# Edge attributes of a graph-attention loop: read by tile number straight from the input, instead of from a staged copy

## The reference

```
x_l = (x @ W_l.T + b_l).reshape(n, 4, 64)
x_r = (x @ W_r.T + b_r).reshape(n, 4, 64)
e_feat = (e_attr @ W_e.T).reshape(-1, 4, 64)
s = leaky_relu(x_l[src] + x_r[dst] + e_feat, 0.2)
alpha = einsum('ehc,hc->eh', s, att)
amax = segment_max(alpha, dst); ex = exp(alpha - amax[dst])
alpha = ex / (segment_sum(ex, dst)[dst] + 1e-16)
out = segment_sum(alpha[..., None] * x_l[src], dst) + bias
h = x + silu(out)
```

## Time and profile before

| what | value |
|---|---|
| time, median of 3 runs | 3392.98 us (3388.5 to 3393.57) |
| the profiled execution, first to last instruction | 3546.6 us |
| edge loop in that execution | about 105 to 1520 us |
| PE busy in the span | 3206.4 us (90%) |
| DVE, ACT, POOL busy | 51%, 39%, 34% |
| bytes moved by DMA in the span | 345.09 MB, 97 GB/s |
| a staged gather, and a store of what it fetched | 56 rows, 448 KB each, 15 times each for both inputs |

### The profile page before, as it was taken

The page is one execution under the profiler, slowest core; times in us unless marked ns, Lnnn a source line. Parts: engine busy times, 40 slices in busy tenths (PEclk is TensorE's granted clock), DMA queues, the critical chain, the costliest instruction groups (busy, mean ns, idle before and its releaser), DMA issues. The chain is left out here.

```text
span 3546.6 us, 52145 instructions
## 1 busy us (share of the span) xinstructions
PE 3206.4 (90%) x14480; PEld 2570.5 (72%) x14481; DVE 1826.2 (51%) x3687; ACT 1387.4 (39%) x4710; POOL 1196.3 (34%) x1148
## 2 busy tenths in 40 slices
PE   6789999999989998957899899889999989999989
PEld 5567776766767676636777777777777778888878
DVE  5666666766766766767353644544373424111002
ACT  2056666666666666663122212312232211222222
POOL 4556666666666666403110310120020001222200
PEclk9899999999999999978999999999999979999999
DMA  7556666665666665533010101000100042333341
GB/s 228 143 146 149 153 149 151 148 147 147 144 147 152 146 149 151 111 100 80 22 43 26 30 8 36 27 8 1 39 24 14 1 156 63 118 117 116 123 134 44
DMA packets 288629, 345.09 MB, mean 97 GB/s; under 512 B 155176, under 2 KB 213655, under 8 KB 284512
## 3 DMA queue, kind: packets, MB, share of 16 engines
q1 hardware_dynamic: 232813, 174.79, 18.5%
q0 software_dynamic: 53632, 157.89, 17.4%
q10 hardware_dynamic: 2064, 10.81, 1.0%
HBM read 298.03 MB, written 44.37 MB: 97 GB/s over the span
## 5 line engine op out<-in xcount | busy, mean ns | idle before, releaser
L1429 POOL DMA_INDIRECT a_g<-xl_d,a_ix x480 | 475.9, 991 | 297.1 <-remote 135.5
L1446 PE MATMUL a_pS<-g_xr,a_lt 128*128 x1680 | 534.8, 401 | 42.5 <-issue 19.4
L1454 PE MATMUL b_pM<-b_m,b_oh 128*112 128x281 f32 x1680 | 457.9, 413 | 23.1 <-DVE g_acc L1585 16.7
L1578 DVE SCALAR_TENSOR_TENSOR a_r<-a_pS,g_attx 128x528 f32<-128x528 f32 x420 | 288.5, 700 | 344.3 <-remote 269.8
L1541 ACT ACTIVATE b_m<-a_g,c_pcx 128x64 f32<-128x64 f32 x1856 | 455.6, 333 | 2.3 <-issue 1.9
L1429 POOL DMA_INDIRECT XS<-xl_d,a_ix x344 | 337.1, 980 | 202.8 <-issue 86.7
L1446 PEld LDWEIGHTS a_pS<-g_xr,a_lt 128*128 128x128 f32 x1680 | 310.3, 193 | 119.6 <-issue 67.2
L1454 PEld LDWEIGHTS b_pM<-b_m,b_oh 128*112 128x112 f32 x1680 | 294.2, 180 | 136.6 <-issue 39.8
L125 POOL TENSOR_TENSOR m_rstd<-m_ve,m_mhalf 125x5 f32<-125x5 f32 x41 | 48.0, 1170 | 902.8 <-DVE m_ve L111 902.8
L1541 ACT ACTIVATE b_m<-XS,c_pcx 128x64 f32<-128x64 f32 x1424 | 349.0, 333 | 1.2 <-issue 1.2
L424 PE MATMUL m_pH<-m_h,m_w 128*128 128x312 f32 (+1 forms) x1280 | 341.9, 428 | 7.7 <-DVE m_h L572 7.7
(11 more groups left out here) (399 smaller groups left out, 4412.6 us busy)
## 6 DMA issues: line engine op xcount, KB each, us to landing
a_db<-dl_d SPq DMA_DIRECT2D x212, 224.0 KB
f_w<-in_ffn_W1p SPq DMA_DIRECT2D x32, 1024.0 KB
m_w<-in_mix_W SPq DMA_DIRECT2D x8, 1024.0 KB
f_w<-in_ffn_W2p SPq DMA_DIRECT2D x8, 1024.0 KB
a_g<-xl_d,a_ix POOLq DMA_INDIRECT x480
a_lt<-eat_d SPq DMA_DIRECT2D x214, 32.0 KB
eat_d<-a_stage SPq DMA_DIRECT2D x15, 448.0 KB
ea_d<-a_stage SPq DMA_DIRECT2D x15, 448.0 KB
```

Source lines behind the costliest of these rows:

```text
L1429: p.indirect_dma_start(out=gathered(t)[:, j, :], out_offset=None, in_=xl_d, in_offset=bass.IndirectOffsetOnAxis(ap=IX[:, t // BSTEPS, n:n ...
L1446: pe.matmul(o, lt[:, j, :], XRW[:, bass.ds(ws[h], 1), :].rearrange("p a d -> p (a d)"), start=True, stop=False)
L1454: ins = pe.matmul(pM[0:WN, h, 0:MW], OH[:, b, j, :], M[:, b, j, :], start=(j == 2 * h), stop=(j == 2 * h + 1))
L1578: v.scalar_tensor_tensor(out=R[:, 2 * h:2 * h + 2, :], in0=pS[0:TE, 2 * h:2 * h + 2, 0:GD], scalar=0.0, in1=attx[:, :].unsqueeze(1).broadc ...
```

## The change

The staged copy goes. The table of tile numbers is loaded once, in the setup, into one row of SBUF (`g_tl`, by way of `tl_d`). In the edge loop SyncE reads the tile number of each pair's first item from that row into a register (`value_load`) and issues a DMA that takes two neighbouring tiles of the input: two DMAs of 16 KB in the place of one of 32 KB, for the transposed attributes and for the others alike. The setup's two gathers and two stores of 1 MB each go, and so do, from each round, the load of 56 tile numbers, the two gathers, the two stores and the waits on them. The input has one tile of padding more. The semaphores `a_eat` and `b_ea` count 32 a step instead of 16.

```diff
--- before
+++ after
...
+        TL = kept("g_tl", [1, ITEMS], I32)
...
-                sp.dma_start(tl_d[0:ITEMS].rearrange("(c p) -> c p", p=128), turned[CH:2 * CH, :]).then_inc(s["i_stored"], 16)
+                sp.dma_start(tl_d.rearrange("(c p) -> c p", p=128), turned[CH:2 * CH, :]).then_inc(s["i_tl_d"], 16)
...
                 xl_part(3)
+                sp.wait_ge(s["i_tl_d"], 16)
+                sp.dma_start(TL[0:1, :], tl_d.unsqueeze(0)).then_inc(s["i_tl"], 16)
...
-                    if q == NG - 2:
-                        a.wait_ge(s["i_ea"], 32)
-                        a.dma_start(eat_d[0:128, :], eaT[:, :]).then_inc(s["i_ea_out"], 16)
-                        a.dma_start(ea_d[0:128, :], ea[:, :]).then_inc(s["i_ea_out"], 16)
...
-                    elif k == 1:
-                        at = bass.IndirectOffsetOnAxis(ap=tile_i[:, 0:1], axis=0)
-                        p.indirect_dma_start(out=eaT[:, :], out_offset=None, in_=g["eaT"], in_offset=at).then_inc(s["i_ea"], 16)
-                        p.indirect_dma_start(out=ea[:, :], out_offset=None, in_=g["ea"], in_offset=at).then_inc(s["i_ea"], 16)
...
+                    def tiles_of(base, c, h):
+                        at = IG * (base + c) + 2 * h
+                        tile = sp.value_load(TL[0:1, (slice(at, at + 1) if isinstance(at, int) else bass.ds(at, 1))], min_val=0, max_val=NTE)
+                        return bass.ds(tile, 2)
+
                     def attributes_of(base, c, k):
-                        sp.dma_start(LT[WN:128, k, :, :], eat_d[four(base, c), :].rearrange("i (c e) -> c i e", c=ED)).then_inc(s[f"a_eat{k}"], 16)
+                        for h in range(2):
+                            sp.dma_start(LT[WN:128, k, 2 * h:2 * h + 2, :],
+                                         g["eaT"][tiles_of(base, c, h), :].rearrange("i (c e) -> c i e", c=ED)).then_inc(s[f"a_eat{k}"], 16)
+
+                    def features_of(base, c, k):
+                        for h in range(2):
+                            sp.dma_start(M[:, k, 2 * h:2 * h + 2, EA0:EA0 + ED],
+                                         g["ea"][tiles_of(base, c, h), :].rearrange("i (e c) -> e i c", c=ED)).then_inc(s[f"b_ea{k}"], 16)
...
-                        if exists(base, t, 0) and t == TILES_AT:
-                            wait(sp, "s_gathered", 32 * i, 0)
-                            sp.dma_start(TIX[:, :], tl_d[staged(i)].unsqueeze(1)).then_inc(s["s_tiles"], 16)
-                        elif exists(base, t, 0) and t == STORE_AT:
-                            sp.wait_ge(s["s_gathered"], 32 * i + 32)
-                            sp.dma_start(eat_d[staged(i), :], STG[:, 0, :]).then_inc(s["s_staged"], 16)
-                            sp.dma_start(ea_d[staged(i), :], STG[:, 1, :]).then_inc(s["s_staged"], 16)
-                        elif exists(base, t, 0) and t == RING - attributes_ahead:
-                            wait(sp, "s_staged", 32 * i, 0)
...
                         if exists(base, t, -WEIGH):
                             wait(sp, "b_summed1", base, t - WEIGH - 1)
-                            sp.dma_start(M[:, t % 2, :, EA0:EA0 + ED], ea_d[four(base, t - WEIGH), :].rearrange("i (e c) -> e i c", c=ED)).then_inc(s[f"b_ea{t % 2}"], 16)
+                            features_of(base, t - WEIGH, t % 2)
...
-                        if t == GATHER_AT:
-                            p.wait_ge(s["s_tiles"], 16 * i + 16)
-                            wait(p, "s_staged", 32 * i, 0)
-                            p.sem_inc(s["a_seen"], 1)
-                            for n, a in enumerate((g["eaT"], g["ea"])):
-                                p.indirect_dma_start(out=STG[:, n, :], out_offset=None, in_=a,
-                                                     in_offset=bass.IndirectOffsetOnAxis(ap=TIX[:, 0:1], axis=0)).then_inc(s["s_gathered"], 16)
...
-                            pe.wait_ge(s[f"a_eat{t % LTS}"], 32 * i + 16 * (t // LTS) + 16)
+                            pe.wait_ge(s[f"a_eat{t % LTS}"], 64 * i + 32 * (t // LTS) + 32)
...
-    ea = np.pad(a["edge_attr_16"], ((0, spare), (0, 0))).reshape(tiles, TE, ED)
+    ea = np.pad(a["edge_attr_16"], ((0, spare + TE), (0, 0))).reshape(tiles + 1, TE, ED)

```

More of the change, by code:

```diff
@@ L48 @@
 ITEMS = 128 * CH
-RI = IG * RING
-STAGED = RI * (ROUNDS + 2)
 ZSLOTS = NT * D // (IG * GD)
@@ L809, in graph_attention @@
 def graph_attention(nc, s, zone, XS, ident, x, xn_d, g, sums_d, scratch, ln1, ln1_of, scale0):
-    key_d, dl_d, eat_d, ea_d, xl_d, wl_d, tl_d, breaks_d, any_d = (scratch[n] for n in ("key", "dl", "eat", "ea", "xl", "wl", "tl", "breaks", "any"))
+    key_d, dl_d, xl_d, wl_d, tl_d, breaks_d, any_d = (scratch[n] for n in ("key", "dl", "xl", "wl", "tl", "breaks", "any"))
     by_head = lambda a: a.rearrange("p (h d) -> p h d", h=GH)
@@ L904, in _ @@
                 sp.dma_start(we[:, :], g["W_e_wide"]).then_inc(s["p_w_e"], 16)
-                sp.wait_ge(s["i_const"], 7)
+                sp.wait_ge(s["i_const"], 6)
                 sp.dma_start(key_d[0:1].unsqueeze(0), edge[0:1, 0:1]).then_inc(s["i_key_d"], 16)
                 sp.dma_start(key_d[ITEMS * TE + 1:ITEMS * TE + 2].unsqueeze(0), edge[0:1, 1:2]).then_inc(s["i_key_d"], 16)
-                sp.dma_start(tl_d[ITEMS:STAGED].unsqueeze(0), beyond[:, :]).then_inc(s["i_stored"], 16)
                 def xl_part(n):
@@ L941, in _ @@
                 sp.wait_ge(s["p_we"], 16)
-                sp.wait_ge(s["i_stored"], 16 * 6)
+                sp.wait_ge(s["i_tl"], 16)
+                sp.wait_ge(s["i_stored"], 16 * 4)
                 sp.wait_ge(s["p_xl_d"], 16 * (NW // XW))
@@ L974, in _ @@
                     a.activation(DLX[:, n * 128:(n + 1) * 128], pX[(CH + n) % 2], ACT.Copy).then_inc(s["i_dl_out"], 1)
-                a.wait_ge(s["i_ea_out"], 32)
                 a.wait_ge(s["p_xn_d"], 32 * NG)
@@ L989, in _ @@
                 p.memset(one28[:, :], 1.0).then_inc(s["i_const"], 1)
-                p.memset(beyond[:, :], NTE).then_inc(s["i_const"], 1)
-                p.wait_ge(s["i_const"], 7)
+                p.wait_ge(s["i_const"], 6)
                 p.affine_select(out=upto[:, :], in_=one28[:, 0:NW], compare_op=ALU.is_ge, fill=0.0, base=0,
@@ L1138, in _ @@
                 v.wait_ge(s["i_ends"], 32)
-                v.wait_ge(s["i_const"], 7)
+                v.wait_ge(s["i_const"], 6)
                 v.tensor_scalar(below[:, 1, :], ends_i[:, 1, :], wbase[:, 0:1], None, ALU.is_lt)
@@ L1272, in graph_attention @@
                 OH = sb("b_oh", [TE, 2, IG, WN])
-                TIX = sb("a_tix", [RI, 1], I32)
-                STG = sb("a_stage", [RI, 2, ED * TE])
                 node = sb("a_node", [128, 1])
@@ L1281, in graph_attention @@
                 block = c.enter_context(nc.Block())
-                TILES_AT, GATHER_AT, STORE_AT = 0, 2, 5
                 def by_item(row):
@@ L1365, in _ @@
                     sp.wait_ge(s["a_const"], 7)
-                    def staged(i):
-                        at = RI * i + 2 * RI
-                        return slice(at, at + RI) if isinstance(at, int) else bass.ds(at, RI)
                     def slot(i, base, t):
-                        if exists(base, t, 0) and t == TILES_AT:
-                            wait(sp, "s_gathered", 32 * i, 0)
-                            sp.dma_start(TIX[:, :], tl_d[staged(i)].unsqueeze(1)).then_inc(s["s_tiles"], 16)
-                        elif exists(base, t, 0) and t == STORE_AT:
-                            sp.wait_ge(s["s_gathered"], 32 * i + 32)
-                            sp.dma_start(eat_d[staged(i), :], STG[:, 0, :]).then_inc(s["s_staged"], 16)
-                            sp.dma_start(ea_d[staged(i), :], STG[:, 1, :]).then_inc(s["s_staged"], 16)
-                        elif exists(base, t, 0) and t == RING - attributes_ahead:
-                            wait(sp, "s_staged", 32 * i, 0)
                         if exists(base, t, 0):
@@ L1401, in _ @@
                     for k in range(LTS):
-                        sp.wait_ge(s[f"a_eat{k}"], 16 * (STEPS // LTS + (k < attributes_ahead)))
+                        sp.wait_ge(s[f"a_eat{k}"], 32 * (STEPS // LTS + (k < attributes_ahead)))
                 @block.gpsimd
@@ L1489, in slot @@
                             wait(pe, "b_onehot", base, t - SUM + 1)
-                            pe.wait_ge(s[f"b_ea{(t - SUM) % 2}"], 112 * (i if t >= SUM else i - 1) + 16 * (ts // 2) + 16)
+                            pe.wait_ge(s[f"b_ea{(t - SUM) % 2}"], 224 * (i if t >= SUM else i - 1) + 32 * (ts // 2) + 32)
                             sums(0)
@@ L2445, in gps_layer @@
         scratch = {"key": dram("key_d", (ITEMS * TE + 2,)), "dl": dram("dl_d", (ITEMS, TE)),
-                   "eat": dram("eat_d", (STAGED, ED * TE)), "ea": dram("ea_d", (STAGED, ED * TE)), "tl": dram("tl_d", (STAGED,), I32),
+                   "tl": dram("tl_d", (ITEMS,), I32),
                    "xl": dram("xl_d", (NW * WN, GD)), "wl": dram("wl_d", (ITEMS,), I32),
@@ L2479, in laid_out @@
```

(6 more changed lines are left out.)

4 lines of the change are left out of this document (removed).

## The result

| | before | changed |
|---|---|---|
| median of 4 runs each, us | 3391.36 (3388.5 to 3393.57) | 3481.47 (3473.35 to 3485.97) |
| ratio, 95% interval | | 1.0269 (1.0257 to 1.0281) |
| span of the profiled execution, us | 3546.6 | 3480.4 (its time: 3482.15) |

The kernel became slower by 90 us, 2.7%. The prediction said 3467 in 3335 to 3690, so the total came out 14 us off. It did not do so by the terms it gave, as the experiments show; the clue is in the table. The changed kernel's profiled execution is as long as its runs, while the one of before was 154 us longer than its runs.

The account below looks back on a forecast made before the run. TensorE was taken to bound the kernel before, SyncE's issuing the changed one: +4.6 us a round, +69 over 15, and 5 at the start make +74 on 3392.98, giving 3467 us, range 3335 to 3690.

Parts of the forecast that it names:

- SyncE becomes the bound: Edge loop: SyncE's issuing, at 97.5 us a round against 88.4 for TensorE, sets the pace; +69 us over 15 rounds.
- What goes, -4.5 us a round: Edge loop: TensorE regains its time lost around the staged gathers, 4.5 us a round, -68 us (-42 to -90).
- the first one: Whole kernel: opening step, reading what bounds it from one profile with span 3546.6 us and TensorE 90% busy.
- the stretch that a profile adds: Whole kernel: unknown extra length of the profiled execution; the difference of +74 us was carried to the median of 3392.98.
- hold-ups: SyncE in the edge loop: delays while issuing, 34 us of issues against up to 62.7 occupied, a factor of 1.84.
- The base of 92.9 us a round: Edge loop before the change: length of a round by the starts of the staged gathers, 92.9 us.
- SyncE's 80.4 us without hold-ups: Changed edge loop: 14 slots of 5.17 us plus 8.0 for small loads, 80.4 us a round, 91% of 88.4.
- The factor of 1.21: Changed edge loop: stretch of SyncE's 80.4 us, a quarter of the way from 1.0 to 1.84, giving 97.5 us.
- Rival 1: Edge loop: SyncE keeps pace, factor below 1.10, TensorE stays the bound and regains 4.5 us a round; 3330 us, chance 27%.
- Slots 2 and 9 lag and catch up: Edge loop: SyncE lags 2.1 us at the six small loads, catches up 1.1 a slot; this lag alone is hidden.
- The setup at 0: Setup: removing 2 MB of gathers and 2 MB of stores gains nothing, counted as 0.
- The eight early loads in pairs: Start of the loop, where first steps are fast: eight issues in pairs cost about 5 us more.

Follow-up runs that it names:

- e2: Changed kernel with a fifth table read in each slot on SyncE, its value unused: 3600.82 us, ratio 1.064.
- e3: Changed kernel without the table reads, the same four two-item transfers a slot addressed from the loop counter: 3381.77 us, ratio 0.9990.
- e5: Changed kernel with both tile numbers of a slot packed into one int, so one table read serves two pairs: 3388.49 us, ratio 0.9997.
- e6: Changed kernel with all four table reads a slot but one transfer of four items in place of two of two: 3384.82 us, ratio 0.9984.
- e4: Kernel before without staging in the loop, attributes of four items loaded by one transfer straight from the input: 3384.70 us, ratio 0.9997.
- e11: e4 also without the setup's gathers and stores of 1 MB, where the kernel before takes 3557.72 us: 3508.42 us, ratio 0.9854.
- e1: Kernel before, unchanged, profiled a second time: 3389.23 us (one run), span 3387.5 us.
- e10: e5 with one more table read in every slot, where the kernel before takes 3557.72 us: 3743.67 us, ratio 1.0536.
- e12: The kernel of e10 once more, where the kernel before takes 3388.56 us: 3397.10 us, ratio 1.0025.
- e8: e5 with the six small loads of slots 2 and 9 spread two by two over three slots each: 3385.71 us, ratio 0.9993.

## Why the prediction was right, and where it was not

**SyncE becomes the bound.** Right, and shown: no waits, idle time ended by `b_m`, e2's 119 us for 14 reads a round, and the loss gone when either the reads (e3, e5) or the halves (e6) go. The changed kernel's 89.0 us a round is SyncE's own. The sizes below are mostly wrong, and that the total still came within 14 us is luck: their errors cancel.

**What goes, -4.5 us a round.** Wrong where the kernel before takes 3387 us: e3 and e4 have it at nothing. The step that failed is the first one, taking for the kernel's normal course. The sign stood in the table of times: a span of 3546.6 beside a median of 3393. The prediction saw it as "the stretch that a profile adds" and carried a difference over; but it changed which engine waits for which. On the chip with those hold-ups the term exists: e11 gained 49 us, inside the bounds of 42 to 90 and below the 68 taken.

**The base of 92.9 us a round.** Wrong by the same step: e1 has 82.4. So TensorE leaves 82.3 and not 88.4 us, and the point from which SyncE decides lies lower.

**SyncE's 80.4 us without hold-ups.** Too low. A slot takes 5.45 us (717.04 to 722.49 in the timeline of the changed kernel) and not 5.17, 3.9 a round; the loop's turn adds 2.7, of which before has 0.3; the two slow reads 0.8; about 1.2 is spread over the rest. Together 89.0.

**The factor of 1.21.** Wrong: it is 1.0 in the changed kernel's own profile, where register moves take 29 to 39 ns, and 1.31 on the chip of e10. Its 17.1 us stood in for 8.6 us of missing prices, and on a base 10.5 us too high. Of its evidence, the long issues belonged to the staging, which goes (e1, e4). Prediction: 97.5 - 92.9 = 4.6 a round. Measured: 89.0 - 82.4 = 6.6. Rival 1, at a factor of 1.0, had forecast 3330 since 80.4 is below 88.4; with the right prices and the right base the same factor gives the slower kernel.

**Slots 2 and 9 lag and catch up.** Right, and more so than stated: at 99% SyncE is still hidden but for 9 us of 3388 (e12), where the prediction counted 91% against it.

**The setup at 0.** Off by some 3 us. In the changed kernel the loop's first load is issued at 96.23 us, in e1 at 99.66:

```profile
99.66 0.36 SPq L1343 DMA_DIRECT2D a_db<-dl_d  x1
```

```profile
96.23 0.35 SPq L1327 DMA_DIRECT2D a_db<-dl_d  x1
```

VectorE's reductions to `a_alpha` divide the rest. In e1 and in the changed kernel:

```profile
L1657 DVE TENSOR_REDUCE a_alpha<-a_r x210: 1226/1247/1255, 111.3 to 1331.0; 128x16 f32<-128x1056 f32 x105
```

```profile
L1632 DVE TENSOR_REDUCE a_alpha<-a_r x210: 1227/1247/1255, 108.0 to 1421.4; 128x16 f32<-128x1056 f32 x105
```

Start -3.3, loop 1313.4 - 1219.7 = +93.7, behind it (3480.4 - 1421.4) - (3387.5 - 1331.0) = +2.5: in all +92.9, the difference of the spans. The eight early loads in pairs, put at 5 us, cost nothing that shows there. The start goes with the setup: the first load is at 95.0 to 98.9 us in the seven other profiles with the change's setup from chips without the hold-ups (e2, e3, e5 to e8, e12) and at 99.5 in e4. That it is the 2 MB of gathers and 2 MB of stores, and not the rest of the setup's edit, is not shown: e11, meant to isolate them, ran on the chip with the hold-ups.

## What to carry to other kernels

Before reading a profile, hold its execution's span against the runs: where it is 4% longer, something behaved otherwise, and neither idle time nor baseline may be taken from it. An engine that only issues has a budget: add up its instructions with gaps, register work and the loop's turn, and compare with the round of the bound engine. Below it, even at 99%, it was nearly free here; above it each microsecond of a round counted in full. Each additional issue and each additional table read cost 0.5 to 0.6 us of the queue here, and half the bytes made an issue no cheaper, so pack several small numbers into one read. And look at the turn of a loop whose body has grown: its program may no longer stay where it is run from.

## What was not expected of the hardware

On one of the four chips of the experiments, and in the first profile of the kernel before, SyncE's instructions, register moves of 29 ns included, took 0.7 us again and again; the kernel before took 3558 us there and 3387 to 3389 on the others. Kernels rank otherwise there: without the staging 1.5% is gained (e11, nearly all in the loop) and not 0.03% (e4), and the kernel of e10 loses 5.4% and not 0.25%. It is SyncE alone, and what causes it the traces don't show. A turn of the loop costs SyncE 0.3 us with up to 250 instructions in the loop and 2.6 to 3.0 with 390 and more, where a packet of instructions comes behind every turn's branch. A table read of 0.27 us takes 0.44 to 0.47 directly behind two of the `c_breaks` loads and 0.66 or more behind those of `c_any`. The two issues behind stores of 448 KB take 1.6 and 2.0 us and not 0.32 (e1). And DMA engines that are 70% busy took nothing from TensorE.
